# 16-wide attention with float32r planes: two rounded parts, two heads in partition halves, planes built per group

## The reference

```python
qkv = einsum('bsh,oh->bso', hidden_states, w_qkv) + b_qkv   # per key head: 4 q, 1 k, 1 v
q = _rope(q, cos, sin); k = _rope(k, cos, sin)
scores = einsum('bqhd,bkhd->bhqk', q, k) / 16
scores = where(mask, scores, finfo.min)                    # causal; at 1024 tokens all blocks are kept
probs = softmax(scores, axis=-1)
ctx = einsum('bhqk,bkhd->bqhd', probs, v).reshape(B, S, 512)
out = einsum('bsh,oh->bso', ctx, w_dense) + b_dense
```

## Time and profile before

| | us |
|---|---|
| median of 2 runs | 2999.4 (2994.22 to 3004.58) |
| the profiled execution | 2997.02 |
| its span, first to last instruction | 2995.0 |
| PE busy (matmul) / weight loads | 2652.2 / 1793.2 |
| DVE, ACT, POOL busy | 1907.5, 1514.3, 822.2 |
| stage L0a, from its first statistics to those of L0f | 9.30 to 486.6 |
| stage L1b, from its first statistics to those of L1g | 2134.3 to 2615.9 |

### The profile page before, as it was taken

One profiled execution on the slowest core, in us unless ns is written; L12 is line 12 of the kernel. 1 busy time (PEld: TensorE's weight loads), 2 busy tenths in 40 slices (PEclk: granted clock), 3 DMA queues, 4 the chain that ended last, 5 costly groups with the idle time before them and its releaser, 6 DMA issues. The chain is left out here.

```text
span 2995.0 us, 46427 instructions
## 1 busy us (share of the span) xinstructions
PE 2652.2 (89%) x14824; PEld 1793.2 (60%) x14886; DVE 1907.5 (64%) x3382; ACT 1514.3 (51%) x2540; POOL 822.2 (27%) x777
## 2 busy tenths in 40 slices
PE   6789988886999999999999987999578888778995
PEld 4444434454888888888888864666344444345663
DVE  5666642444777787777777766677556666166774
ACT  4466661222555555555555541566265666324663
POOL 1200000104343443445335301455120000003552
PEclk9799998997999999999999988999788999979998
DMA  2100000001000000000000023988500000029887
GB/s 76 71 1 0 0 1 16 19 17 46 19 22 22 22 22 18 22 22 26 15 22 25 8 92 135 297 201 199 144 1 1 0 0 0 11 107 322 211 201 197
DMA packets 68154, 196.92 MB, mean 66 GB/s; under 512 B 9040, under 2 KB 9936, under 8 KB 62608
## 3 DMA queue, kind: packets, MB, share of 16 engines
q1 hardware_dynamic: 46928, 145.44, 14.2%
q0 software_dynamic: 21056, 49.30, 8.7%
HBM read 154.33 MB, written 40.37 MB: 65 GB/s over the span
## 5 line engine op out<-in xcount | busy, mean ns | idle before, releaser
L1315 ACT ACTIVATE L1a_ph<-single 128x512 fp32r<-128x512 f32 (+3 forms) x384 | 174.2, 489 | 180.4 <-PE single L1402 179.7
L698 DVE TENSOR_REDUCE L1b_least<-single 128x1 f32<-128x512 f32 (+3 forms) x304 | 191.2, 660 | 107.9 <-PE single L520 75.9
L698 DVE TENSOR_REDUCE L0a_least<-single 128x1 f32<-128x512 f32 (+3 forms) x304 | 191.1, 660 | 106.9 <-PE single L520 75.5
L1456 DVE TENSOR_TENSOR L1a_pl<-single,L1a_ph 128x512 fp32r<-128x512 f32 (+3 forms) x384 | 199.5, 549 | 52.7 <-ACT L1a_ph L1315 52.0
L1472 DVE SCALAR_TENSOR_TENSOR x<-single,L1a_rinv,x 128x512 f32<-128x512 f32 x256 | 189.5, 745 | 58.4 <-PE single L1066 58.4
L1306 ACT ACTIVATE L1a_probs<-pair,L1a_least 128x128 f32<-128x128 f32 (+7 forms) x256 | 190.0, 744 | 72.0 <-DVE L1a_least L1450 70.8
L1450 DVE TENSOR_REDUCE L1a_least<-pair 128x1 f32<-128x128 f32 (+7 forms) x256 | 190.8, 750 | 43.3 <-PE pair L1391 42.6
L1283 POOL TENSOR_TENSOR L1a_swapped<-L1a_swapped,L1a_sin 128x512 f32<-128x512 f32 x80 | 129.8, 1622 | 303.7 <-ACT L1a_swapped L1347 303.7
L409 ACT ACTIVATE L1b_probsT<-pair 128x896 f32<-128x896 f32 (+2 forms) x192 | 151.2, 811 | 67.4 <-PE pair L539 48.1
L409 ACT ACTIVATE L0a_probsT<-pair 128x896 f32<-128x896 f32 (+2 forms) x192 | 151.2, 811 | 65.9 <-PE pair L539 46.5
L1402 PE MATMUL single<-ident,L1a_probs 128*128 128x128 f32 x1152 | 169.0, 274 | 1.4 <-ACT L1a_probs L1306 1.4
(11 more groups left out here) (517 smaller groups left out, 7052.1 us busy)
## 6 DMA issues: line engine op xcount, KB each, us to landing
L1f_wd<-in_L1f_w SPq DMA_DIRECT2D x48, 512.0 KB, 4.3
L1g_wd<-in_L1f_w SPq DMA_DIRECT2D x48, 512.0 KB, 4.2
L1a_raw<-in_L1a_w SPq DMA_DIRECT2D x80, 256.0 KB, 2.6
L1f_store<-in_L1f_w SPq DMA_DIRECT2D x16, 1024.0 KB, 7.9
L1g_store<-in_L1f_w SPq DMA_DIRECT2D x16, 1024.0 KB, 8.4
sum<-L0a_pad_row SPq DMA_DIRECT2D x2, 2304.0 KB, 11.7
sum<-x SPq DMA_DIRECT2D x16, 256.0 KB, 2.9
x<-sum SPq DMA_DIRECT2D x16, 256.0 KB, 4.7
```

The source lines that it names most:

```text
L698: dve.tensor_reduce(a.least[:, part, qt, first:first + heads], g.bank(4 + f % 2)[:, 0:heads * w].rearrange("p (j k) -> p j k", j=heads), A ...
L1315: act.activation(p_tile(ph, u, i), turned_bank(u, i), ACT.Copy).then_inc(p_high, 1)
L1456: dve.tensor_tensor(p_tile(pl, u, i), turned_bank(u, i), p_tile(ph, u, i).bitcast(F32), ALU.subtract)\
```

## The change

Both 16-wide stages, and nothing else, change.

- **Two rounded parts in float32r instead of three in bfloat16.** A number is its float32r rounding plus the rest: three products, 48 rows (`KF`), and two rows more for the maximum (`KM` = 50).
- **Two heads in partition halves.** `qs` and `ks` give a head 64 partitions (`ROWS16`); a plane of `qT` holds heads 0 and 1, or 2 and 3, and `kT` the key twice. A matmul takes rows 0 to 49 or 64 to 113.
- **Planes built per group.** The turning of stacks in the projections is gone, with `first_parts`, `later_parts` and `stack_copy`. POOL builds the parts of a group by half (`build`: six instructions), two groups ahead; PE turns a plane of four tiles (`turn_plane`, four float32r matmuls with the identity, bank 7) and ACT copies it (`plane_copy`, 128x512). A group has ten planes: K and two Q for either half, and the two Q again for either half with the maximum in it (M); those replace the eight `row` steps.
- **Straight code.** The loops become Python loops, and addresses constants.
- **Minima between turned scores.** A fill of the next group, of heads in the other partition half where there is one, stands between the two matmuls of a unit. There are now 40 fills per group (two heads of like parity share one).
- POOL's `output_bias` moves behind the first groups' builds.

```diff
+        now = []
+        while len(left) > 2 and given + len(left[0][2]) * left[0][3] <= total * (n + 1) / NU:
+            now.append(next_fill((j + 1 + len(now)) % 2))
...
+                    pool.tensor_tensor(ks[:, :, :, 0:HD], k, like(2, HD), ALU.mult).then_inc(a.stack_high, 1)
+                    pool.tensor_tensor(qs[:, :, :, 0:HD], q, like(GH, HD), ALU.mult).then_inc(a.stack_high, 1)
+                    pool.tensor_tensor(ks[:, :, :, HD:2 * HD], k, like(2, HD), ALU.mult).then_inc(a.stack_high, 1)
+                    pool.tensor_tensor(qs[:, :, :, 2 * HD:KF], q, like(GH, HD), ALU.mult).then_inc(a.stack_high, 1)
+                    pool.wait_ge(a.stack_high, 4 * n + 4)
+                    pool.tensor_tensor(ks[:, :, :, 2 * HD:KF], k, ks[:, :, :, 0:HD].bitcast(F32), ALU.subtract)\
+                        .then_inc(a.stacked, 1)
+                    pool.tensor_tensor(qs[:, :, :, HD:2 * HD], q, qs[:, :, :, 0:HD].bitcast(F32), ALU.subtract)\
+                        .then_inc(a.stacked, 1)
...
+                def plane_copy(kind, kv, p, c):
+
+                    cols = slice(c * HALF, (c + 1) * HALF)
+                    to = a.kT[:, kv % SETS, cols] if kind == "K" else a.qT[:, kv % SETS, p, cols]
+                    act.wait_ge(a.plane_turned, PLANE[kind, kv, p, c])
+                    act.activation(to, g.bank(7), ACT.Copy).then_inc(a.plane_copied, 1)
...
-                def turn_stack(t):
...
+                    for i in range(BLK):
+                        t, b = c * BLK + i, kv % SETS
+                        rows = a.ks[:, kv % 2, t, :, :] if kind == "K" else a.qs[:, b, t, 2 * p:2 * p + 2, :]
+                        mm = pe.matmul(g.bank(7)[:, i * P:(i + 1) * P], rows.rearrange("p j d -> p (j d)"), a.ident[:, :],
+                                       start=True, stop=True)
+                    mm.then_inc(a.plane_turned, 1)
...
+                        r, k = ROWS16 * (j % 2), part * HALF
+                        mm = pe.matmul(fill_bank(kv, f)[:, n * w:(n + 1) * w],
+                                       a.qT[r:r + KF, kv % SETS, j // 2, qt * P:(qt + 1) * P],
+                                       a.kT[r:r + KF, kv % SETS, k:k + w], start=True, stop=not last)
...
+                    for n, kt in enumerate((pair, pair + 1)):
                         q = first_query(c, kt)
-                        out = g.pair[u % 2][:, o:o + HALF - q]
...
+                        if n and o < HALF:
+                            mask(0)
+                        outs.append(g.pair[u % 2][:, o:o + HALF - q])
+                        mm = pe.matmul(outs[n], a.kT[r:r + KM, b, kt * P:(kt + 1) * P],
+                                       a.qT[r:r + KM, b, j // 2, c * HALF + q:(c + 1) * HALF], start=True, stop=not diagonal)
                         o += HALF - q
...
+                        if n < len(ahead):
+                            if n:
+                                fill_mask(kv + 1, ahead[0], len(FILLS[ahead[0]][2]) - 1)
+                            fill(kv + 1, ahead[n])
...
-                with pe.Fori(0, NKV - 1) as kv:
-                    group(kv, True)
-                group(NKV - 1, False)
```

More of the change, by code:

```diff
@@ L201, in fills @@
             w = min(HALF, (qt + 1) * P - part * HALF)
-            n = max(1, min(GH, HALF // w))
-            out += [(qt, part, j, n, w) for j in range(0, GH, n)]
+            pairs = ((0, 2), (1, 3)) if 2 * w <= HALF else ((0,), (1,), (2,), (3,))
+            out += [(qt, part, heads, w) for heads in pairs]
     return out
@@ L209, in groups @@
     return [(c, kt) for c in range(2) for kt in range(0, BLK * (c + 1), 2)]
-FILLS, GROUPS = fills(), groups()
-NF, NG = len(FILLS), len(GROUPS)
-NF0 = sum(f[0] < BLK for f in FILLS)
+GROUPS = groups()
+NG = len(GROUPS)
 NU = NG * GH
@@ L221, in first_query @@
     return max(0, kt - BLK * c) * P
+TURNS_AT = {
+    2: ("M", 0, 0, 1), 4: ("M", 0, 1, 1), 6: ("K", 2, 0, 0), 8: ("Q", 2, 0, 0), 10: ("Q", 2, 1, 0),
+    13: ("M", 1, 0, 0), 15: ("M", 1, 1, 0), 17: ("K", 2, 0, 1), 19: ("Q", 2, 0, 1), 21: ("Q", 2, 1, 1),
+}
 def heads16_plan():
[L226 to L258, removed]
+    left, order, plan = fills(), [], []
+    total, given = sum(len(h) * w for _, _, h, w in left), 0
+    def next_fill(parity):
+        block = [f for f in left if f[0] // BLK == left[0][0] // BLK][:GH]
+        f = next((f for f in block if f[2][0] % 2 == parity), block[0])
+        left.remove(f)
+        order.append(f)
+        return len(order) - 1
@@ new lines, in heads16_plan, with heads16_start @@
+    plan += [("fill", next_fill(0)), ("weigh", NG - 1), ("copy", 1), ("fill", next_fill(1)), ("turn", 1)]
+    return plan, order
+PLAN16, FILLS = heads16_plan()
+NF = len(FILLS)
+NF0 = sum(f[0] < BLK for f in FILLS)
+def heads16_start():
+    first = [("K", 0, 0, 1), ("Q", 0, 0, 1), ("Q", 0, 1, 1)]
+    later = [("M", 0, 0, 0), ("M", 0, 1, 0)] + [(k, 1, p, c) for c in range(2) for k, p in (("K", 0), ("Q", 0), ("Q", 1))]
+    out = [("plane", "K", 0, 0, 0), ("plane", "Q", 0, 0, 0), ("plane", "Q", 0, 1, 0)]
+    for f in range(NF):
+        out.append(("fill", f))
+        if f < NF0 and f % 3 == 2 and first:
+            out.append(("plane", *first.pop(0)))
+        if f >= NF0 + 2 and f % 3 == 2 and later:
+            out.append(("plane", *later.pop(0)))
+    return out + [("plane", *p) for p in first + later]
```

469 lines of the change are left out of this document (236 added, 233 removed).

## The result

The changed kernel takes 3333.9 us (median of two runs, 3332.9 to 3334.9) against 2999.4: 1.112 times the time, 95% interval 1.103 to 1.120. It is 11% slower; I had forecast 2922 and a range that ended at 3062.

A forecast was written before the change was run, and what follows sets the result against it. PE was taken to bound the loop. Saving 34.7 us ahead of it in each stage (69.4) and 0.4 in each of 14 turns (5.6) took 2997.0 to 2922.0 us; range 2843 to 3062.

The forecast's parts named there:

- Projections and first planes: Ahead of the loop: without stack turning the last projection ends at 67.5 us and the first fill stands at 72.4.
- First fills: Ahead of the loop: 40 reductions with ten planes between take 30.5 us, so the first unit starts at 104.0.
- lower bound of 28 us: Least gain per stage ahead of the loop, if PE with planes at low clock becomes slower than DVE; 34.7 forecast.
- fifth rival: Ahead of the loop: low-clock PE and POOL's builds hold the fills, 28 us gained instead of 34.7, 13 us in all; no own chance.
- Packing: In the loop: a fill runs beside a unit on the other partition half, hiding about 4.0 of 17.4 us a turn.
- Changing shape: In the loop: 46 entries into half rows a turn at 0.08 us, 3.7 us, plus 1.4 for `weigh`.
- the column price of 0.24: Highest of three bounds for a shape change in the loop: 0.24 us per round trip into and out of the column shape.
- rivals 3 and 4: In the loop: half rows cost what columns cost, 3031 us (chance 0.18); the same without packing, 3087 us (0.13).
- Waiting: In the loop: of 6.3 us PE waiting a turn about 3.7 stay, the chain at a group's end and ACT.
- The clock in the loop: In the loop: granted clock is 1.00 now and PE stays as busy; no time or rival was given for a fall.
- rival 3: In the loop: half rows cost what columns cost, 46 round trips at 0.24 us, a turn of 46.4, 3031 us; chance 0.18.
- my signs: Profile checks: first unit about 104 us, packing starts, shape price, turn length, one table load; wrong if turn under 36 or over 42.

The follow-up runs named there:

- Full rows: Changed kernel with every fill and score matmul over all 128 rows, the keys' plane kept twice with zero halves, masks in bfloat16: 2977.2 us, 0.993 of before.
- early planes: Kernel with all matmuls over 128 rows, its first three plane turns moved between the last projections: 2978.2 us, 0.994 of before; same move with half rows: 3321.1 us.
- added matmuls: 128-row kernel with first plane turns between the last projections, plus 55 matmuls that nobody reads in the fills ahead of the loop: 2949.2 us, 0.984 of before.
- full-height scores: Changed kernel with only the score matmuls over all 128 rows, the fills staying 48 rows high: 3380.4 us (one run).

## Why the prediction was wrong

**Which stage.** The first unit came 16.05 us later than forecast in the first stage (120.05 against 104.0), 15.3 in the second: 31. From the first unit to the last turn of the context in group 6, seven turns took 454.2 and 448.0 us (64.9 and 64.0 each) instead of 7 x 39.1 in either stage: 355. The last groups took 45.6 and 42.0 instead of 30.0 and 31.7: 26. These are 412 of the 413 us between 2922.0 and 3334.9, the time of the profiled execution.

**Projections and first planes: right.** The last projection was to end at 67.5; PE's timeline of the kernel after has it at 57.90 + 10.48 = 68.4, and the first fill at 73.63, where I put 72.4.

**First fills: the wrong engine's pace.** I gave them 31.6 us; they took 46.4. The failed step is "I put at 30.5": I had scaled the 28.1 us of the kernel before, which is DVE's pace. These are the fills of the kernel before, then those of the kernel after, in windows:

```profile
109.50:137.60 28.10, 24.43 (x88) 7.26 (x85) 23.82 (x38) 1.91 (x4) 1.24 (x5) 0.50 0.47 173
73.60:120.00 46.40, 44.30 (x124) 25.31 (x124) 24.51 (x39) 7.85 (x12) 9.98 (x20) 0.50 0.31 114
```

The clock was already at 0.50 in the kernel before, of which the prediction has no row; there PE (24.4 us busy) just kept up with DVE (23.8). With float32r fills and planes at the same clock PE was busy 44.3 us, and DVE still 24.5. Full rows at 0.50 take 39.3 (76.2 to 115.5), so 7 of the 15 us too many go with the half rows; at 1.00, with early planes and added matmuls, they take 33.8 (69.7 to 103.45), near my figure. My lower bound of 28 us and fifth rival had the mechanism (planes at the low clock make PE slower than DVE) but sized it at 13 us for two stages; it was 31.

**Packing: right.** A fill starts beside the unit within 0.01 us, and two 512-wide matmuls take 0.34 us together at full clock where two at full height take 0.46. I took 4.0 us a turn; no run shows its worth at full clock. At the clock as it was, taking it away cost 10.

**Changing shape: mis-sized by three.** "I take 0.08 per entry" is the failed step. At full clock a 512-wide fill with a mask on either side takes 0.15 + 0.44 us at half height (237.20, 237.35 and 237.79 above). At the same place of the order, at full height, in the kernel with added matmuls, it takes 0.04 + 0.32:

```profile
220.70 0.23 PE L577 MATMUL single<-mask_b,ident_b 128*128 128x128 bf16 x1
220.74 0.47 PE L568 MATMUL single<-L0a_kT,L0a_qT 128*128 128x512 f32 x1
221.06 0.28 PE L593 MATMUL pair<-ident_b,mask_b 128*128 128x128 bf16 x2
```

So a round trip costs 0.11 + 0.12 = 0.23 us around a mask; between long matmuls without a mask it is 0.35 (0.15 in, 0.20 out, the timeline of full-height scores above). The first is the column price of 0.24, which I had as the highest bound and gave to rivals 3 and 4: 46 x 0.23 = 10.6 us a turn instead of 3.7. The reason I gave for the low value, that half rows are nearer in kind to 96 rows than to columns, was wrong. The rule I had cited against my own value, from the Trainium skill, TensorEngine Tiling (Array Packing), Key Properties, names such a change of mode as a drain, and the trace agrees that it costs time, 0.11 to 0.20 us each way.

**Waiting: at full height too low by about 2.** Without half rows and without packing my sum for a turn is 34.3 + 3.7 + 1.4 = 39.4; the full-rows kernel took 41.7. The waits of its weight loads, in the kernel with added matmuls over six turns:

```profile
PEld single L568 <- DVE L0a_least L751: 15.2, 52, 0.6
```

2.5 us a turn are waits for DVE's minima, which I had not counted, since DVE is busy only 26 us of the turn. That short fills come two behind each other faster than it reduces them is my reading, not shown. In the changed kernel PE hardly waited at all (0.2 of 389 us).

**The clock in the loop: the largest miss.** "In the loop it is 1.00 now, and PE stays as busy" is the failed step that outweighs the others: one sentence without a rival beside it, where the clock came to 0.64 (0.66 in the second stage). What the turn would have taken at full clock can be read from the same stretch of the order, 13 us between two `weigh`, in two kernels that both had 1.00 there: the changed kernel, then the one at full height with added matmuls.

```profile
228.42 0.50 PE L594 MATMUL pair<-L0a_qT,L0a_kT 50*128 50x512 f32 x1
...
241.01 3.14 PE L625 MATMUL single<-L0a_probsT,L0a_vg 128*32 128x512 f32 x16
```

```profile
212.01 0.44 PE L600 MATMUL pair<-L0a_qT,L0a_kT 128*128 128x512 f32 x1
...
223.84 1.71 PE L631 MATMUL single<-L0a_probsT,L0a_vg 128*32 128x512 f32 x16
```

12.59 us against 11.83, 6% more. If the rest of the turn behaves as this stretch, the changed kernel at 1.00 needs (12.59 / 11.83) x 41.8 = 44.5 us a turn, an estimate: 5 more than forecast, near rival 3's 46.4. Measured were 64 to 65. So some 20 us a turn, 280 in all, are the clock's; the other 75 are the dearer changes of shape (6.9 us a turn more than I took), less the waiting that did not come. The whole would then have come to about 3000 to 3030, near rival 3 and inside my range. The split is worked out, not measured: no run has half rows at full clock throughout.

**What I had asked the profile.** Of my signs the packing and the single table load of the stage came about as written, and so did the busy times of ACT (154.0 / 6 = 25.7 us a turn) and DVE (27.1); POOL took 7.0 instead of 9. "Wrong if the turn is over 42" and "if the first unit comes after 112 us" both held. No sign asked for the granted clock of the loop.

**What is shown and what isn't.** Shown: the half-height matmuls bring the loop's clock down (1.00 without them; 0.57 to 0.72 in every kernel with them); neither float32r, nor the masks, nor the overlap does it. Ahead of the loop idle time does it, and added work holds it up. Not settled: by which property the half rows do it. Added full-height work raised the clock and less overlap lowered it, as if what counted were how much of the array works over time; but masks that stream twice as long lowered it to 0.58, which that reading does not explain. The other reading, that the time lost in changes of shape counts as idle, has more against it: without masks the changes fall from some 50 a turn to 18 and the clock is no higher, while the kernel before lost 3.9 us to idle time and 3.4 to changes of shape out of 39 (19%) and kept 1.00. The Trainium skill, TensorE: Matmul & The Clock Gate, Part 1, ties the clock to how busy the engine is and warns of idle gaps. The fills ahead of the loop agree that it falls in a gap. In the loop the profile shows no idle PE (388.82 of 389 us busy) and a clock of 0.64, so there a busy PE in the profile's sense does not hold it.

## What to carry to other kernels

Price half-height matmuls by three terms: the overlap won (0.46 to 0.34 us for two 512-wide ones), the change of shape (0.23 us a round trip around a mask, 0.35 without one), and a clock that may fall. Here the first two nearly cancelled at full clock, and the third decided. With the masks gone they still did not pay: 52.2 us a turn, against 41.7 at full height with all masks. Two zero halves in the stationary operand keep two heads apart at full height, for one more copy a plane of keys, and here turned 3334 us into 2977. And wherever PE waits on another engine ahead of a dense loop, look at the granted clock, not at the busy share: early planes and matmuls that nobody reads took the rest of the way to 2949, 1.6% under the kernel before; 22 of these 28 us went with the added matmuls.

## What the runs showed of the hardware that I had not expected

- PE is shown as busy while it changes shape: a loop with 100% busy PE had its engines waiting (DVE 36.5 us a turn) and ran at 0.64 of the clock, while the same loop at full height, 97% busy, ran at 1.00.
- At half clock a bfloat16 mask holds the half-height matmul behind it off for 0.22 us, a float32r mask for 0.40, and the exchange cost 13.5 us a turn of 64 masks; at full height the same exchange cost 0.8.
- 55 added matmuls in the start of a stage made it faster: first score matmul at 103.45 instead of 112.2 us.
- The kernel before ran its first fills at half clock too (109.5 to 137.6 us), without losing by it, as DVE set the pace there.
